# Two of three head-sum tiles added up before TensorE, and the rows of pi read back for two bands

## The chip, the cores and the metric

One core of one Trainium2 chip runs the whole problem in one launch. The metric is device time in microseconds, the median of three runs. A profiled execution shows what each engine did: PE (TensorE), DVE (VectorE), ACT (ScalarE), POOL (GpSimd) and SP (SyncE, which here issues most DMAs).

## The reference

```python
x = x + _L0_conv_ref(_gn(x), qkv_w, temp, out_w, out_b)   # x: (32, 384, 32, 32), 12 heads of 32 channels
...
    w = jnp.einsum('bnc,oc->bno', xt, qkv_w).reshape(b, n, HEADS, d).transpose(0, 2, 1, 3)
    norm = jnp.sqrt(jnp.sum(w * w, axis=-2, keepdims=True))
    w_normed = w / jnp.maximum(norm, 1e-12)
    s = jnp.sum(w_normed * w_normed, axis=-1)
    Pi = jax.nn.softmax(s * temp[None, :, :], axis=1)
    Pi_n = Pi / (jnp.sum(Pi, axis=-1, keepdims=True) + 1e-08)
    dots = jnp.einsum('bhn,bhnd->bhd', Pi_n, w * w)[:, :, None, :]
    attn = 1.0 / (1.0 + dots)
    out = -(w * Pi[..., None]) * attn
    out = jnp.einsum('bnc,oc->bno', out, out_w) + out_b
```

`_gn` is a group norm over 32 groups. For each image there are two products of 384 x 384 weights with 384 x 1024 values. Between them stands a softmax over the 12 heads at each of the 1024 positions. Its score of a head is the sum over the head's 32 channels of the squares, each channel's squares divided by their sum over the positions.

## The kernel before

The 32 images run one after the other in a software pipeline. An image's 384 channels are three tiles of 128 partitions (t = 0, 1, 2), each with 1024 positions in the free dimension. In each tile the 128 partitions are the 32 channels of four heads, so tile 0 holds heads 0 to 3, tile 1 heads 4 to 7 and tile 2 heads 8 to 11. Each product is written as three products of a high and a low part of weights and data (XH and XL, UH and UL, W1H and so on).

The order of the work is written out by hand: every engine has its own list of instructions, and semaphores hold them together. In `step(i)`:

- PE makes the three tiles of the first product of image i (`first_product`), then those of the second product of image i - 1 (`second_product`). `head_sums(i)` stands inside the second product of tile 0. It streams the squares of each tile against a column per head, `headsum[:, t, :]`, in four matmuls for the four quarters of the partitions of `scores`.
- ACT squares each tile of the first product (`square_w`, which also leaves the sums over the positions in `sumsq`), keeps the tile itself (`keep_w`), makes the high part of the weighed values of image i - 1 (`u_hi`) and normalises image i + 1 (`normalise`, `x_hi`).
- DVE first ends image i - 2 (`finish`, L1149), then works on image i - 1: three dot products (`dot`, L1041), the little chain of `attention` (L1053 and on), three weighings (`weigh`, L1067) and the low parts (`u_lo`, L1141). Then come the moments of the group norm of image i + 1 (L937), `head_sum_weights(i)` (L990 to L996), `group_norm`, the third `u_lo`, statistics (L906), the softmax of image i (L1005 to L1033) and the ends of image i - 1.
- SP stores image i - 2, loads image i + 2, and in `spread_pi(i)` sends the softmax out to DRAM and reads it back so that every partition has the rows of its head:

```python
                    for t in tiles:
                        rows = pi_dram[t * HPT:(t + 1) * HPT].rearrange("h (b q n) -> q (h b) n", b=BLOCKS, q=QUADS)
                        sp.dma_start(rows, PIT[:, t, :]).then_inc(pi_written[t], 16)
                    for t in tiles:
                        sp.wait_ge(pi_written[t], rows_moved(j, t, 16))
```

The writes are L375 and the reads, into PIB[:, t], L380. The dot products and the weighings of the next step use these rows. For the first and the last image the rows of tile 0 are spread by PE transposes instead (`spread_heads`), and the tiles are weighed one at a time (`attend_tile`, L1041, L1080, L1101).

Of the kernel before, what the change touches and what calls it, by code (L numbers as in the profile page):

```python
# [33 lines left out]
P = 128  # L34
# [6 lines left out]
QUAD = 32  # L41
# [4 lines left out]
BY_MATMUL = 3  # L46
HEADSUM_STEPS = 3
IDLE_TURNS = (4, 4)
SM_SHIFTED, SM_STEPS = 3, 8
ATTENDED = 3 + 4  # L50
U_STEPS = ATTENDED + 3
# [32 lines left out]
def conv_attention(nc, x, qkv_w, temp, out_w, out_b, y):  # L84
# [4 lines left out]
    T = C // P  # L89
    HPT = P // D  # L90
    HALVES = N // BANK
    BLOCKS = N // P
# [7 lines left out]
    with ExitStack() as ctx:  # L100
# [51 lines left out]
        srec = sb("srec", [P, BLOCKS])  # L152
        pi_part = sb("pi_part", [P, HPT])
        pi_heads = sb("pi_heads", [P, BLOCKS, HPT])
        PIT = sb("PIT", [P, T, QUAD + 1])
        PIB = sb("PIB", [P, T, BLOCKS * QUADS, QUAD + 1])
        pick = sb("pick", [P, T, HEADS])
# [45 lines left out]
        w_kept = sem("w_kept")  # L203
        headsum_step = sem("headsum_step")
        scores_done = sem("scores_done")
# [3 lines left out]
        pi_spread = [sem(f"pi_spread_{t}") for t in range(T)]  # L209
        u_step = sem("u_step")  # L210
# [50 lines left out]

        def rows_moved(j, t, more=0):

            return j.counts(16, more - (16 if t == 0 and True else 0))

# [74 lines left out]
        def _(sp):  # L340
# [67 lines left out]
        def _(pool):  # L408
# [6 lines left out]
            pool.wait_ge(w2_loaded, 16)  # L415
            pool.tensor_copy(mixed_w2.rearrange("p (m d h) -> p m d h", d=D, h=HPT),
                             raw_w2.rearrange("p (m h d) -> p m d h", d=D, h=HPT)).then_inc(w2_mixed, 1)

# [34 lines left out]
        def _(act):  # L453
# [83 lines left out]
            def widen_heads(j):  # L537

                act.wait_ge(heads_kept, pe_spread(j))
                if j.follows(1):  # L540
                    act.wait_ge(u_step, (j - 1).counts(U_STEPS, 1))
                act.activation(wide_heads(j).rearrange("p (b d h) -> p b d h", b=BLOCKS, d=D),
                               pi_heads[:].unsqueeze(2).to_broadcast([P, BLOCKS, D, HPT]), ACT.Copy)\
# [62 lines left out]
            def x_hi_first():  # L606
# [19 lines left out]
            act.wait_ge(u_step, last.counts(U_STEPS, 2 - U_STEPS))  # L626
            act.activation(wide_part(last).rearrange("p (d h) -> p d h", d=D),
                           pi_part[:].unsqueeze(1).to_broadcast([P, D, HPT]), ACT.Copy).then_inc(heads_widened, 1)
            u_hi(last, 0)
# [13 lines left out]
        def _(pe):  # L643
            def turn_weights(ks):
# [3 lines left out]
                for k in ks:  # L648
                    for m in range(T):
                        raw = columns1[:, k, m, :] if k < T else columns2[:, k - T, m, :]  # L650
                        if k < T:
                            into = turned(k)[:, m * P:(m + 1) * P].rearrange("p (d h) -> p h d", h=HPT)
# [136 lines left out]
            def head_sums(i):  # L789
# [5 lines left out]
                if i.follows(1):  # L795
                    pe.wait_ge(sm_step, i.counts(SM_STEPS))
                for t in range(T):
                    for q in range(QUADS):
                        block_q = square_tile(i, t).rearrange("p (b q r) -> p q b r", q=QUADS, r=QUAD)[:, q]
                        last = pe.matmul(scores[q * QUAD:(q + 1) * QUAD, 0:N // QUADS], headsum[:, t, :],  # L800
                                         block_q, start=(t == 0), stop=(t == T - 1))
                last.then_inc(scores_done, 1)
# [42 lines left out]
            def turn_w2():  # L845

                pe.wait_ge(w2_mixed, 1)
                pe.wait_ge(temp_kept, 1)
# [19 lines left out]
        def _(dve):  # L868
# [115 lines left out]
            def head_sum_weights(j):  # L984

                if not has(j):
                    return
                link = chain(headsum_step, j.counts(HEADSUM_STEPS))
                dve.wait_ge(squared, j.counts(T, T))
                link(dve.tensor_scalar(inv[:, 0, :], sumsq[:], NORM_FLOOR ** 2, None, ALU.max))  # L990
                link(dve.reciprocal(inv[:, 1, :], inv[:, 0, :]))
# [4 lines left out]
                link(dve.tensor_tensor(headsum[:], head_temp[:],  # L996
                                       inv[:, 1, :].unsqueeze(2).to_broadcast([P, T, QUAD]), ALU.mult), follows=False)

# [12 lines left out]
            def softmax_divide(j):  # L1011
# [7 lines left out]
                if by_pe(j):  # L1019
                    dve.tensor_tensor(pi_heads[:], EX[:, :, 0:HPT],  # L1020
                                      srec[:].unsqueeze(2).to_broadcast([P, BLOCKS, HPT]), ALU.mult).then_inc(heads_kept, 1)
                    if j.follows(1):
# [5 lines left out]
                if j.follows(1):  # L1028
                    for t in range(T):
                        if j.follows(2) or rows_moved(j, t) > 0:  # L1030
                            dve.wait_ge(pi_written[t], rows_moved(j, t))
                link(dve.transpose(PIT[:, :, 0:QUAD], scores[:, P:P + HEADS * BLOCKS]))
                link(dve.tensor_reduce(PIT[:, :, QUAD], PIT[:, :, 0:QUAD], AX_X, ALU.add), follows=False)  # L1033

            def dot(j, t):

                if has(j):
                    dve.wait_ge(pi_spread[t], rows_moved(j, t, 16))
                    dve.wait_ge(squared, j.counts(T, t + 1))
                    dve.wait_ge(scores_done, j.counts(1, 1))  # L1040
                    dve.tensor_tensor_reduce(in_blocks(square_tile(j, t)), PIB[:, t, :, 0:QUAD],  # L1041
                                             in_blocks(square_tile(j, t)), 1.0, 0.0,
                                             ALU.mult, ALU.add, dots[:, 0, t:t + 1]).then_inc(u_step, 1)

            def attention(j, k):
# [4 lines left out]
                if k > 0:  # L1050
                    dve.wait_ge(u_step, j.counts(U_STEPS, T + k))
# [10 lines left out]
            def weigh(j, t):  # L1062

                if has(j):
                    dve.wait_ge(u_step, j.counts(U_STEPS, ATTENDED))
                    dve.wait_ge(w_kept, j.counts(T, t + 1))
                    dve.scalar_tensor_tensor(in_blocks(w_tile(j, t)), in_blocks(w_tile(j, t)), dots[:, 3, t:t + 1],  # L1067
                                             PIB[:, t, :, 0:QUAD], ALU.mult, ALU.mult).then_inc(u_step, 1)

            def attend_tile(j, t, within=()):  # L1070
# [15 lines left out]
                else:  # L1086
                    rows = PIB[:, t, :, 0:QUAD]
                    dot(j, t)
                    dve.tensor_reduce(total, PIB[:, t, :, QUAD], AX_X, ALU.add).then_inc(tile_step, 1)
                for other in within:  # L1090
# [61 lines left out]
            def step(i):  # L1152
# [36 lines left out]
            def head_columns(t):  # L1189

                dve.tensor_reduce(head_mask[:, t, t * HPT:(t + 1) * HPT],
                                  identity[:].rearrange("p (d h) -> p h d", h=HPT), AX_X, ALU.add).then_inc(heads_set, 1)

# [83 lines left out]
```

## Time and profile before

| | |
|---|---|
| Time, median of 3 runs | 867.25 us (867.11 to 867.55) |
| Span of the profiled execution | 864.9 us |
| PE busy in it | 851.6 us (98%) |
| DVE busy | 750.2 us (87%) |
| ACT busy | 528.3 us (61%) |
| POOL busy | 232.6 us (27%) |
| TensorE clock granted | full speed in all 40 slices |

The span is the only time that the profile gives of the profiled execution: from its first to its last instruction. The time of a run is some 2.4 us longer than that span. Rows give the start and the duration in microseconds from the start of the span, and a name such as `WS<-PIB,WS` says which tile is written and which are read.

### The profile page before, as it was taken

How to read it: one execution, taken by the hardware profiler on the slowest of the kernel's cores; microseconds unless marked ns; L12 is line 12 of the kernel's file. 1: busy time of each engine (PE TensorE's matmuls, PEld its weight loads, DVE VectorE, ACT ScalarE, POOL GpSimd, SP SyncE). 2: the span in 40 equal slices, each digit the busy share in tenths (PEclk: the TensorE clock that was granted, in tenths of full speed). 3: DMA queues.
4: the chain of work that ended last, by engine and by line, in shares of the span. 5: the costliest groups of instructions: out<-in, count | busy, mean ns of one | idle time of the engine just before them, and what ended most of it. 6: DMA issues, size and time to landing. Idle time of an engine off the chain costs nothing.

```text
span 864.9 us, 14022 instructions
## 1 busy us (share of the span) xinstructions
PE 851.6 (98%) x4290; PEld 677.7 (78%) x4290; DVE 750.2 (87%) x1396; ACT 528.3 (61%) x680; POOL 232.6 (27%) x106
## 2 busy tenths in 40 slices
PE   7999999999999999999999999999999999999997
PEld 6767788777787777787777787777887777887776
DVE  7989889898888888888888898888898888898777
ACT  3567656567555677556676556676565675566642
POOL 2432123332123331133331233321233321233300
PEclk9999999999999999999999999999999999999999
DMA  7324665544664544664535654445655446645225
GB/s 279 119 79 153 225 229 185 185 148 169 225 227 161 197 146 181 226 223 160 180 150 198 228 213 168 163 145 220 227 186 196 141 163 225 228 175 186 88 86 197
DMA packets 45259, 157.42 MB, mean 182 GB/s; under 512 B 19866, under 2 KB 23962, under 8 KB 37274
## 3 DMA queue, kind: packets, MB, share of 16 engines
q1 hardware_dynamic: 36856, 154.10, 48.5%
q10 hardware_dynamic: 8354, 2.85, 1.3%
q14 instruction: 40, 0.33, 0.1%
q8 instruction: 9, 0.15, 0.1%
HBM read 104.47 MB, written 52.45 MB: 181 GB/s over the span
## 4 chain that ended last, share of the span: by engine, by line
PE 92%; DVE 4%; issue 1%; DMA 1%; ACT 1%; DVEq 0%; ACTq 0%
PE acc L678 86%; PE spread_ps L800 5%; DVE stats L906 1%; DVE WS L1041 1%; DMA PIB<-pi 0%; DMA X<-in_x 0%; DVE WV L1101 0%; DVE X L1149 0%; PE acc L655 0%; DVE WS L1080 0%; ACT WS L501 0%; DMA pi<-PIT 0%; DVE X L1116 0%; ACT WV L512 0%; PE spread_ps L815 0%
## 5 line engine op out<-in xcount | busy, mean ns | idle before, releaser
L424 POOL TENSOR_TENSOR XL<-XN,XH 128x1024 fp32r<-128x1024 f32 x93 | 222.9, 2414 | 571.7 <-ACT XH L529 548.2
L501 ACT ACTIVATE WS<-acc 128x1024 f32<-128x1024 f32 x96 | 98.4, 1026 | 240.5 <-PE acc L678 197.1
L678 PE MATMUL acc<-XH,W1H 128*128 128x512 f32 x574 | 177.3, 390 | 0.1
L678 PE MATMUL acc<-XH,W1L 128*128 128x512 f32 x574 | 176.8, 389 | 0.0
L678 PE MATMUL acc<-UH,W2H 128*128 128x512 f32 x558 | 172.6, 390 | 1.3 <-ACT WV L512 1.2
L678 PE MATMUL acc<-UH,W2L 128*128 128x512 f32 x558 | 172.3, 390 | 0.0
L678 PE MATMUL acc<-XL,W1H 128*128 128x512 f32 x576 | 146.2, 389 | 0.0
L678 PE MATMUL acc<-UL,W2H 128*128 128x512 f32 x558 | 145.3, 396 | 0.0
L1149 DVE SCALAR_TENSOR_TENSOR X<-acc,bias,X 128x1024 f32<-128x1024 f32 x93 | 116.3, 1276 | 31.0 <-PE acc L678 31.0
L678 PEld LDWEIGHTS acc<-UL,W2H 128*128 128x128 f32 x558 | 102.3, 188 | 32.2 <-issue 11.9
L678 PEld LDWEIGHTS acc<-XL,W1H 128*128 128x128 f32 x576 | 108.0, 188 | 22.7 <-POOL XL L434 0.3
L678 PEld LDWEIGHTS acc<-XH,W1L 128*128 128x128 f32 x574 | 107.7, 188 | 22.5
L678 PEld LDWEIGHTS acc<-XH,W1H 128*128 128x128 f32 x574 | 107.3, 188 | 23.0 <-issue 0.9
L678 PEld LDWEIGHTS acc<-UH,W2H 128*128 128x128 f32 x558 | 104.3, 188 | 24.9 <-issue 2.1
L1041 DVE CUSTOM_DVE_ANT_0 WS<-PIB,WS 128x1024 f32<-128x1024 f32 x94 | 113.5, 1222 | 10.2 <-DMA PIB<-pi 8.1
L906 DVE BATCH_NORM_STATS2 stats<-X 128x6 f32<-128x512 f32 x192 | 120.0, 680 | 2.5 <-DMA X<-in_x 2.5
L678 PEld LDWEIGHTS acc<-UH,W2L 128*128 128x128 f32 x558 | 104.6, 188 | 22.4 <-issue 0.4
L491 ACT ACTIVATE UH<-WV 128x1024 fp32r<-128x1024 f32 x93 | 95.0, 1054 | 41.7 <-DVE WV L1067 37.5
L519 ACT ACTIVATE XN<-X,norm 128x1024 f32<-128x1024 f32 x91 | 112.3, 1235 | 0.4 <-DVE XN L961 0.4
L1141 DVE TENSOR_TENSOR UL<-WV,UH 128x1024 fp32r<-128x1024 f32 x93 | 111.2, 1222 | 0.1
L1067 DVE SCALAR_TENSOR_TENSOR WV<-WV,dots,PIB 128x1024 f32<-128x1024 f32 x90 | 110.3, 1281 | 1.1
L529 ACT ACTIVATE XH<-X,norm 128x1024 fp32r<-128x1024 f32 x90 | 111.0, 1233 | 0.0
(119 smaller groups left out, 501.3 us busy)
## 6 DMA issues: line engine op xcount, KB each, us to landing
PIB<-pi SPq DMA_DIRECT2D x94, 528.0 KB, 5.1
X<-in_x SPq DMA_DIRECT2D x31, 1536.0 KB, 6.3
out_y<-X SPq DMA_DIRECT2D x30, 1536.0 KB, 6.5
gathered<-stats_rows ACTq DMA_DIRECT2D x28, 72.0 KB, 5.1
pi<-PIT SPq DMA_DIRECT2D x94, 16.5 KB
X<-in_x SPq DMA_DIRECT2D x3, 512.0 KB, 4.7
out_y<-X SPq DMA_DIRECT2D x1, 1024.0 KB, 6.0
out_y<-X SPq DMA_DIRECT2D x2, 512.0 KB, 2.6
```

What stands on the lines that cost most here:

```text
L424: pool.tensor_tensor(XL[:, t, :], XN[:, t, :], XH[:, t, :].bitcast(F32), ALU.subtract).then_inc(xl_done, 1)
L491: act.activation(u_tiles(j)[0][:, t, :], w_tile(j, t), ACT.Copy).then_inc(uh_done, 1)
L501: act.activation(square_tile(i, t), acc[:, t, :], ACT.Square, accum_out=sumsq[:, t:t + 1]).then_inc(squared, 1)
L519: act.activation(XN[:, t, :], x_tile(j, t), ACT.Identity, bias=shift_j, scale=rstd_j).then_inc(xn_done, 1)
L529: act.activation(XH[:, t, :], x_tile(j, t), ACT.Identity, bias=shift_j, scale=rstd_j).then_inc(xh_done, 1)
L678: last = pe.matmul(out[:, h * BANK:(h + 1) * BANK], w[:, k, m * P:(m + 1) * P], r[:, k, h * BANK:(h + 1) * BANK], start=(n == 0 and k == 0 ...
L800: last = pe.matmul(scores[q * QUAD:(q + 1) * QUAD, 0:N // QUADS], headsum[:, t, :], block_q, start=(t == 0), stop=(t == T - 1))
L906: last = dve.bn_stats(stats[:, k, :], X[:, j.slot, k * BANK:(k + 1) * BANK])
L1041: dve.tensor_tensor_reduce(in_blocks(square_tile(j, t)), PIB[:, t, :, 0:QUAD], in_blocks(square_tile(j, t)), 1.0, 0.0, ALU.mult, ALU.add, ...
L1067: dve.scalar_tensor_tensor(in_blocks(w_tile(j, t)), in_blocks(w_tile(j, t)), dots[:, 3, t:t + 1], PIB[:, t, :, 0:QUAD], ALU.mult, ALU.mult ...
L1141: dve.tensor_tensor(low[:, t, :], w_tile(j, t), high[:, t, :].bitcast(F32), ALU.subtract).then_inc(ul_done[t], 1)
L1149: dve.scalar_tensor_tensor(x_tile(j, t), acc[:, t, :], bias[:, t:t + 1], x_tile(j, t), ALU.add, ALU.add).then_inc(y_done, 1)
```

## The change

In every image from the third on, the squares of tiles 0 and 1 are added up before PE sees them, each scaled by the inverse of its channel's sum (`inv`). For this the two tiles get one common layout, in which the 128 partitions are 16 channels of eight heads in each tile ("band 0", heads 0 to 7), so that a partition belongs to the same head in both. Tile 2 stays as it is ("band 1"). The columns of the first and the rows of the second weight matrix are reordered at the start to suit.

- DVE makes the scales of tiles 0 and 1 early (`pair_weights`, after the three weighings).
- ACT writes scaled squares of tile 0 to a new tile `paired` (`scale_first`, ahead of the third square).
- DVE adds the scaled squares of tile 1 (`add_second`, after `group_moments` and ahead of `head_sum_weights`, which is left with tile 2).
- PE streams `paired` and tile 2: eight matmuls in the code instead of twelve.
- SP writes the softmax out in three DMAs as before, but reads it back in two: one for band 0, once writes 0 and 1 have landed, and one for band 1. Tiles 0 and 1 use the same rows.
- The sum over the rows in `attention` becomes two instructions. In the first and last image PE spreads eight heads instead of four, and all three tiles are written out.

```diff
                     sp.wait_ge(sm_step, j.counts(SM_STEPS, SM_STEPS))
-                    tiles = range(1 if by_pe(j) else 0, T)
-                    for t in tiles:
+                    for t in range(T):
                         rows = pi_dram[t * HPT:(t + 1) * HPT].rearrange("h (b q n) -> q (h b) n", b=BLOCKS, q=QUADS)
                         sp.dma_start(rows, PIT[:, t, :]).then_inc(pi_written[t], 16)
-                    for t in tiles:
-                        sp.wait_ge(pi_written[t], rows_moved(j, t, 16))
-                        heads = pi_dram[t * HPT:(t + 1) * HPT].unsqueeze(0)\
-                            .to_broadcast([D, HPT, BLOCKS * QUADS * (QUAD + 1)])
-                        sp.dma_start(PIB[:, t].rearrange("p b n -> p (b n)"), heads).then_inc(pi_spread[t], 16)
+                    for band, of_band in enumerate(BAND_HEADS):
+                        for t in range(of_band.start // HPT, of_band.stop // HPT):
+                            sp.wait_ge(pi_written[t], j.counts(16, 16))
+                        heads = pi_dram[of_band.start:of_band.stop].unsqueeze(0)\
+                            .to_broadcast([P // len(of_band), len(of_band), BLOCKS * QUADS * (QUAD + 1)])
+                        sp.dma_start(PIB[:, band].rearrange("p b n -> p (b n)"), heads).then_inc(pi_spread[band], 16)
...
+            def scale_first(i):
+
+                if has(i):
+                    act.wait_ge(headsum_step, i.counts(HEADSUM_STEPS, 2))
+                    act.wait_ge(squared, i.counts(T, 1))
+                    act.wait_ge(scores_done, i.counts(1))
+                    act.activation(paired[:], square_tile(i, 0), ACT.Copy, scale=inv[:, 1, 0:1]).then_inc(pair_step, 1)
...
                 square_w(i, 1)
                 u_hi(i - 1, 1)
                 u_hi(i - 1, 2)
+                scale_first(i)
                 square_w(i, 2)
...
-                for t in range(T):
+                if paired_sums(i):
+                    pe.wait_ge(pair_step, i.counts(PAIR_STEPS, PAIR_STEPS - PAIR_STEPS * PAIRED))
+                    streams = [(head_temp[:, 0, :], paired[:]), (headsum[:, T - 1, :], square_tile(i, T - 1))]
+                else:
+                    streams = [(headsum[:, t, :], square_tile(i, t)) for t in range(T)]
+                for n, (weights, squares) in enumerate(streams):
...
+            def pair_weights(j):
+
+                if not has(j):
+                    return
+                link = chain(headsum_step, j.counts(HEADSUM_STEPS))
+                dve.wait_ge(squared, j.counts(T, 2))
+                dve.wait_ge(scores_done, j.counts(1))
+                link(dve.tensor_scalar(inv[:, 0, 0:2], sumsq[:, 0:2], NORM_FLOOR ** 2, None, ALU.max))
+                link(dve.reciprocal(inv[:, 1, 0:2], inv[:, 0, 0:2]), follows=False)
+
+            def add_second(j):
+
+                if not has(j):
+                    return
+                dve.wait_ge(pair_step, j.counts(PAIR_STEPS, 1 - PAIR_STEPS * PAIRED))
+                dve.scalar_tensor_tensor(paired[:], square_tile(j, 1), inv[:, 1, 1:2], paired[:], ALU.mult, ALU.add)\
+                    .then_inc(pair_step, 1)
...
-                    dve.wait_ge(pi_spread[t], rows_moved(j, t, 16))
+                    dve.wait_ge(pi_spread[BAND[t]], j.counts(16, 16))
...
-                    done = dve.tensor_reduce(total, PIB[:, :, :, QUAD], AX_X, ALU.add)
+                    dve.tensor_reduce(total[:, 0:2], PIB[:, 0, :, QUAD].unsqueeze(1).to_broadcast([P, 2, BLOCKS * QUADS]),
+                                      AX_X, ALU.add).then_inc(u_step, 1)
+                    done = dve.tensor_reduce(total[:, 2:3], PIB[:, 1, :, QUAD], AX_X, ALU.add)
...
                 weigh(i - 1, 2)
+                pair_weights(i)
                 u_lo(i - 1, 0)
                 u_lo(i - 1, 1)
                 group_moments(i + 1)
+                add_second(i)
                 head_sum_weights(i)
```

## Rows read from the trace of the kernel before

**Rows 1.** The page, busy time of each engine.

```profile
PE 851.6 (98%) x4290; PEld 677.7 (78%) x4290; DVE 750.2 (87%) x1396; ACT 528.3 (61%) x680; POOL 232.6 (27%) x106
```

**Rows 2.** The chain that ended last, 400 to 455 us: start, us, what.

```profile
416.72 1.43 PE spread_ps L800 x24
418.15 24.72 PE acc L678 x108
```

**Rows 3.** Waits of DVE, 89 to 796 us: total us, times, longest.

```profile
DVE X L1149 <- PE acc L678: 24.9, 28, 0.9
DVE inv L990 <- ACT WS L501: 19.6, 23, 1.0
...
DVE WS L1041 <- DMA PIB<-pi: 8.1, 16, 1.0
```

**Rows 4.** Timeline of DVE: first dots of images 1, 2, 29; end of a softmax.

```profile
64.88 1.22 DVE L1041 CUSTOM_DVE_ANT_0 WS<-PIB,WS 128x1024 f32<-128x1024 f32 x1
...
82.67 0.26 DVE L1033 TENSOR_REDUCE PIT<-PIT 128x3 f32<-128x96 f32 x1
...
89.16 1.22 DVE L1041 CUSTOM_DVE_ANT_0 WS<-PIB,WS 128x1024 f32<-128x1024 f32 x1
...
795.30 1.22 DVE L1041 CUSTOM_DVE_ANT_0 WS<-PIB,WS 128x1024 f32<-128x1024 f32 x1
```

**Rows 5.** Timeline of SP's DMA issues, image 2.

```profile
82.95 1.71 SPq L375 DMA_DIRECT2D pi<-PIT  x3
85.11 1.89 SPq L380 DMA_DIRECT2D PIB<-pi  x3
```

**Rows 6.** Landing of single first reads at 85.1, 424.5, 790.6 us; of all reads.

```profile
PIB<-pi SPq DMA_DIRECT2D x1, 528.0 KB, 4.0
...
PIB<-pi SPq DMA_DIRECT2D x1, 528.0 KB, 4.2
...
PIB<-pi SPq DMA_DIRECT2D x1, 528.0 KB, 4.3
...
DMA to landing us min/median/max: 3.8/5.1/6.8
```

**Rows 7.** Timeline of DVE, 407 to 418 us.

```profile
407.71 3.68 DVE L1067 SCALAR_TENSOR_TENSOR WV<-WV,dots,PIB 128x1024 f32<-128x1024 f32 x3
...
411.30 2.35 DVE L1141 TENSOR_TENSOR UL<-WV,UH 128x1024 fp32r<-128x1024 f32 x2
...
415.34 0.17 DVE L990 TENSOR_SCALAR inv<-sumsq 128x3 f32<-128x3 f32 x1 [0.96 <-ACT WS L501]
...
415.54 0.18 DVE L991 RECIPROCAL inv<-inv 128x3 f32<-128x3 f32 x1
...
416.84 0.21 DVE L953 TENSOR_SCALAR norm<-group_mv,norm 128x1 f32<-128x1 f32 x1
...
417.01 1.23 DVE L1141 TENSOR_TENSOR UL<-WV,UH 128x1024 fp32r<-128x1024 f32 x1
```

**Rows 8.** Groups by line and shape: busy us, mean ns | idle before.

```profile
L1053 DVE TENSOR_REDUCE pi_tot<-PIB 128x3 f32<-128x96 f32 x30 | 9.9, 331 | 0.0
...
L1089 DVE TENSOR_REDUCE pi_tot<-PIB 128x1 f32<-128x32 f32 x4 | 0.8, 207 | 0.0
...
L491 ACT ACTIVATE UH<-WV 128x1024 fp32r<-128x1024 f32 x93 | 95.0, 1054 | 41.7 <-DVE WV L1067 37.5 <-DVE WV L1101 4.2
...
L519 ACT ACTIVATE XN<-X,norm 128x1024 f32<-128x1024 f32 x91 | 112.3, 1235 | 0.4 <-DVE XN L961 0.4
```

**Rows 9.** Timeline of ACT, 411 to 415 us.

```profile
411.13 2.00 ACT L491 ACTIVATE UH<-WV 128x1024 fp32r<-128x1024 f32 x2
...
414.19 1.03 ACT L501 ACTIVATE WS<-acc 128x1024 f32<-128x1024 f32 x1 [1.07 <-PE acc L678]
```

**Rows 10.** Timeline of DVE, the last image: end of softmax, dot of tile 1.

```profile
839.08 0.26 DVE L1033 TENSOR_REDUCE PIT<-PIT 128x3 f32<-128x96 f32 x1
...
845.71 1.21 DVE L1041 CUSTOM_DVE_ANT_0 WS<-PIB,WS 128x1024 f32<-128x1024 f32 x1
```

More of the change, by code:

```diff
@@ L46 @@
 BY_MATMUL = 3
-HEADSUM_STEPS = 3
+HEADSUM_STEPS = 5
+PAIR_STEPS = 2
+PAIRED = 2
+BAND = (0, 0, 1)
+BANDS = 2
 IDLE_TURNS = (4, 4)
 SM_SHIFTED, SM_STEPS = 3, 8
-ATTENDED = 3 + 4
+ATTENDED = 3 + 5
 U_STEPS = ATTENDED + 3
@@ L90, in conv_attention @@
     HPT = P // D
+    PAIR_HEADS = 2 * HPT
+    PAIR_D = P // PAIR_HEADS
+    BAND_HEADS = (range(0, PAIR_HEADS), range(PAIR_HEADS, HEADS))
     HALVES = N // BANK
@@ L152, in conv_attention @@
         srec = sb("srec", [P, BLOCKS])
-        pi_part = sb("pi_part", [P, HPT])
-        pi_heads = sb("pi_heads", [P, BLOCKS, HPT])
+        pi_part = sb("pi_part", [P, PAIR_HEADS])
+        pi_heads = sb("pi_heads", [P, BLOCKS, PAIR_HEADS])
+        paired = sb("paired", [P, N])
         PIT = sb("PIT", [P, T, QUAD + 1])
-        PIB = sb("PIB", [P, T, BLOCKS * QUADS, QUAD + 1])
+        PIB = sb("PIB", [P, BANDS, BLOCKS * QUADS, QUAD + 1])
         pick = sb("pick", [P, T, HEADS])
@@ L204, in conv_attention @@
         headsum_step = sem("headsum_step")
+        pair_step = sem("pair_step")
         scores_done = sem("scores_done")
@@ L208, in conv_attention @@
         pi_written = [sem(f"pi_written_{t}") for t in range(T)]
-        pi_spread = [sem(f"pi_spread_{t}") for t in range(T)]
+        pi_spread = [sem(f"pi_spread_{band}") for band in range(BANDS)]
         u_step = sem("u_step")
@@ L260, in pe_spread, with band_rows, paired_sums @@
             return 2 if j.follows(1) else 1
-        def rows_moved(j, t, more=0):
-            return j.counts(16, more - (16 if t == 0 and True else 0))
+        def band_rows(t):
+            return PIB[:, BAND[t], :, 0:QUAD]
+        def paired_sums(j):
+            return j.follows(PAIRED)
         def tile_steps(j, t, steps):
@@ L415, in _ @@
             pool.wait_ge(w2_loaded, 16)
-            pool.tensor_copy(mixed_w2.rearrange("p (m d h) -> p m d h", d=D, h=HPT),
-                             raw_w2.rearrange("p (m h d) -> p m d h", d=D, h=HPT)).then_inc(w2_mixed, 1)
+            for band in BAND_HEADS:
+                columns, h = slice(band.start * D, band.stop * D), len(band)
+                pool.tensor_copy(
+                    mixed_w2.rearrange("p (t c) -> p t c", t=T)[:, :, columns].rearrange("p t (d h) -> p t d h", h=h),
+                    raw_w2.rearrange("p (t c) -> p t c", t=T)[:, :, columns].rearrange("p t (h d) -> p t d h", h=h))\
+                    .then_inc(w2_mixed, 1)
             def x_lo(j, t):
@@ L626, in _ @@
             act.wait_ge(u_step, last.counts(U_STEPS, 2 - U_STEPS))
-            act.activation(wide_part(last).rearrange("p (d h) -> p d h", d=D),
-                           pi_part[:].unsqueeze(1).to_broadcast([P, D, HPT]), ACT.Copy).then_inc(heads_widened, 1)
+            act.activation(wide_part(last).rearrange("p (d h) -> p d h", d=PAIR_D),
+                           pi_part[:].unsqueeze(1).to_broadcast([P, PAIR_D, PAIR_HEADS]), ACT.Copy).then_inc(heads_widened, 1)
             u_hi(last, 0)
@@ L651, in turn_weights @@
                         if k < T:
-                            into = turned(k)[:, m * P:(m + 1) * P].rearrange("p (d h) -> p h d", h=HPT)
+                            band = BAND_HEADS[m * HPT // PAIR_HEADS]
+                            heads = slice(m * HPT - band.start, (m + 1) * HPT - band.start)
+                            into = turned(k)[:, band.start * D:band.stop * D].rearrange("p (d h) -> p h d", h=len(band))[:, heads]
                         else:
@@ L796, in head_sums @@
                     pe.wait_ge(sm_step, i.counts(SM_STEPS))
-                for t in range(T):
+                if paired_sums(i):
[4 more added lines that the diff above has]
+                for n, (weights, squares) in enumerate(streams):
                     for q in range(QUADS):
-                        block_q = square_tile(i, t).rearrange("p (b q r) -> p q b r", q=QUADS, r=QUAD)[:, q]
-                        last = pe.matmul(scores[q * QUAD:(q + 1) * QUAD, 0:N // QUADS], headsum[:, t, :],
-                                         block_q, start=(t == 0), stop=(t == T - 1))
+                        block_q = squares.rearrange("p (b q r) -> p q b r", q=QUADS, r=QUAD)[:, q]
+                        last = pe.matmul(scores[q * QUAD:(q + 1) * QUAD, 0:N // QUADS], weights, block_q,
+                                         start=(n == 0), stop=(n == len(streams) - 1))
                 last.then_inc(scores_done, 1)
@@ L845, in turn_w2 @@
             def turn_w2():
[L847 removed]
+                pe.wait_ge(w2_mixed, BANDS)
                 pe.wait_ge(temp_kept, 1)
@@ L987, in head_sum_weights @@
                     return
-                link = chain(headsum_step, j.counts(HEADSUM_STEPS))
+                tiles = slice(T - 1, T) if paired_sums(j) else slice(0, T)
+                done = HEADSUM_STEPS - 3 if paired_sums(j) else 0
+                link = chain(headsum_step, j.counts(HEADSUM_STEPS, done))
                 dve.wait_ge(squared, j.counts(T, T))
-                link(dve.tensor_scalar(inv[:, 0, :], sumsq[:], NORM_FLOOR ** 2, None, ALU.max))
-                link(dve.reciprocal(inv[:, 1, :], inv[:, 0, :]))
+                link(dve.tensor_scalar(inv[:, 0, tiles], sumsq[:, tiles], NORM_FLOOR ** 2, None, ALU.max))
+                link(dve.reciprocal(inv[:, 1, tiles], inv[:, 0, tiles]))
                 if j.follows(1):
@@ L995, in head_sum_weights @@
                     dve.wait_ge(temp_kept, 3)
-                link(dve.tensor_tensor(headsum[:], head_temp[:],
-                                       inv[:, 1, :].unsqueeze(2).to_broadcast([P, T, QUAD]), ALU.mult), follows=False)
+                weights = headsum[:, tiles, :]
+                dve.tensor_tensor(weights, head_temp[:, tiles, :], inv[:, 1, tiles].unsqueeze(2).to_broadcast(weights.shape),
+                                  ALU.mult).then_inc(headsum_step, HEADSUM_STEPS - 2 - done)
+            def pair_weights(j):
[12 more added lines that the diff above has]
+                    .then_inc(pair_step, 1)
             def softmax_shift(j):
@@ L1086, in attend_tile @@
                 else:
-                    rows = PIB[:, t, :, 0:QUAD]
+                    rows = band_rows(t)
                     dot(j, t)
-                    dve.tensor_reduce(total, PIB[:, t, :, QUAD], AX_X, ALU.add).then_inc(tile_step, 1)
+                    dve.tensor_reduce(total, PIB[:, BAND[t], :, QUAD], AX_X, ALU.add).then_inc(tile_step, 1)
                 for other in within:
```

22 lines of the change are left out of this document (11 added, 11 removed).

## The prediction

> **What bounds the kernel now.** I read four views. First the busy line of the page: the matmul engine (PE) is busy for 851.6 of 864.9 us, DVE for 750.2 [rows 1]. Second the chain of work that ended last, over two periods of the loop: it is PE alone, 1.43 us of head sums and 24.72 us of products, which makes a period of 26.15 us [rows 2]. The first dot product on DVE is at 89.16 for image 2 and at 795.30 for image 29 [rows 4]: 706.14 us / 27 = 26.15 as well. So whatever shortens PE shortens the kernel, as long as nothing else needs 26.15 us.
>
> Third, therefore, what DVE waits for in those 27 periods [rows 3]. It idles 24.9 us for PE before the last store tile and 19.6 us for ACT's third square before the head sum weights. These 44.5 us, 1.65 a period, are real slack. But 16 times it also idles for the rows of pi that come back from DRAM: those rows already arrive only just in time. That is a second loop beside PE's: dot products, weighing, head sum weights, softmax, rows written out, rows read back, dot products of the next image.
>
> Fourth, that loop measured by itself. One period shows its DVE part with no wait for PE, ACT or DMA ahead of the head sum weights: from the first dot at 64.88 to the end of the last softmax reduction at 82.67 + 0.26 = 82.93 [rows 4], so 18.05 us. Behind it the writes are issued at 82.95, the first read at 85.11 [rows 5], it lands 4.0 us later [rows 6], and the dot starts at 89.16 [rows 4]. Loop: 18.05 + 6.23 = 24.28 us against 26.15. The slack is 1.87 us, and what the change adds to this loop is to be held against it.
>
> **The change part by part.** *PE.* 24 head sum records take 1.43 us [rows 2], three tiles of eight; one tile goes, 1.43 / 3 = 0.48 us. PE's period would be 25.67. All 30 paired images together could give 14.3 us.
>
> *ACT.* scale_first writes 128x1024 from SBUF. The plain copy of that shape takes 1.05 us, the one with scale and bias operands 1.24 [rows 8]; I take 1.1. It stands where ACT now idles 1.07 us before the third square (copies end at 411.13 + 2.00, the square starts at 414.19) [rows 9], so it costs nothing on the path. If it ran 0.2 over, the third square would be as late, and behind it the seeds and w copies; DVE reaches the weights later than before anyway (below), which covers that.
>
> *DVE, pair_weights.* Two small linked instructions after the last weighing: 0.20 from the first to the second (415.34 to 415.54), and from a small one to the next subtraction 0.17 (416.84 to 417.01) [rows 7]. 0.37 us; bounds 0.30 (some of it overlapped) and 0.45 (a wait instruction not hidden). Its wait for the second square is met: ACT squares tile 1 right after copying the first weighed tile, 1 us each, while DVE still weighs two tiles. Behind pair_weights stand the two subtractions, and scale_first waits for it too.
>
> *DVE, add_second.* Same instruction and shape as the weighing: three take 411.30 - 407.71 = 3.59, so 1.20 us [rows 7] (1.28 if nothing overlaps). Behind it in DVE's order are the head sum weights, the group norm, the third subtraction and the softmax, so all of it is in the loop.
>
> *DVE, small ones.* The reduction of totals becomes two, of 64 and 32 elements instead of 96. 96 take 0.33, 32 take 0.21 [rows 8]: I take +0.07; bounds nothing and a whole instruction, 0.21. The weights of one tile instead of three go from 96 to 32 elements, which in the reductions is worth 0.12 [rows 8]; I take -0.07, bounds -0.10 and 0.
>
> Sum on DVE: 0.37 + 1.20 + 0.07 - 0.07 = 1.57 us; bounds 1.40 and 1.94. That alone is most of the 1.87.
>
> *The rows.* Three writes stay. The reads become two of the same 528 KB. The third read disappears, which helps only the third dot: the first dot, which starts the chain, now waits for band 0, and SP may issue that only after writes 0 **and** 1. Writes go out 1.71 / 3 = 0.57 to 0.6 us apart [rows 5], so the first read leaves 0.6 us later than now: 85.11 - 82.93 = 2.18 becomes 2.78 (bounds 2.75, and 2.87 if SP needs a further wait instruction). From issue to landing the first read of an image took 4.0, 4.2 and 4.3 us in the first, 14th and last of 28 periods [rows 6]; the mean of the 28 is 4.1. With 0.02 to the dot, the way from softmax to first dot is 2.78 + 4.1 + 0.02 = 6.90 us, against 6.23 in the measured period. Bounds: 2.75 + 3.8 (the least of all reads [rows 6]) + 0.02 = 6.57, and 2.87 + 4.3 + 0.02 = 7.19.
>
> On this price the Trainium skill would come out otherwise. Its page "DMA: Bandwidth & Descriptors", section "Anatomy of one DMA", fits a transfer as 2.0 us plus its bytes at 436 GB/s, fitted on the GpSimd path, while this read is SP's. For 528 KB that is an estimate of 3.24 us; the trace does not agree, with 4.0 to 4.3 [rows 6], and the measurement decides.
>
> *Start and end.* The weights' copy in two pieces, the strided transposes and the head masks move the same elements once; one more instruction is worth 0.2 [rows 8], and I take nothing. The last image has tile 1 waiting for band 0: now its dot starts at 845.71, 6.37 us after 839.34 [rows 10], and 6.8 to 6.9 are needed, so +0.5. Image 29 to 30 has no statistics to make, and runs at PE's shorter period, -0.5; the last head sums give 0.4 back. Together -0.4.
>
> **The sum.** Let s be what DVE adds plus the way of the rows: 1.57 + 6.90 = 8.47. The loop's period is 18.05 + 8.47 = 26.52 us, longer than PE's 25.67 and than today's 26.15. PE then idles 0.85 us an image at the head sums. The first dot of image 2 moves from 89.16 to 64.88 + 26.52 = 91.40, +2.24; 27 periods give 27 x (26.52 - 26.15) = +10.0; the ends -0.4. Total +11.8. In general: (s - 6.23) + 27 (s - 8.10) - 0.4. On the profiled execution that is 864.9 + 11.8 = 876.7 of span; the median of the runs, 867.25, lies 2.4 above that span, which I take as unchanged: 879.
>
> Bounds: s = 1.40 + 6.57 = 7.97 gives -2.2, 865; s = 1.94 + 7.19 = 9.13 gives +30.3, 897.6.
>
> **The rivals.**
>
> 1. *The second write costs nothing* (other side: faster). If band 0 lands when the first read lands today, 6.25 us behind the softmax, s is 7.82 and the loop 25.87: 1.6 - 7.6 - 0.4 = -6.4, 861. It decides from s = 8.05, that is from a way below 6.5 us; below 6.05 PE at 25.67 is the bound again. For it: the stretch before the landing is the same, and if something other than the issue set it, the issue would not move it. Against: 4.0 to 4.3 us from issue in three periods [rows 6], so the issue moves the landing. Chance 0.10. The page of the Trainium skill named above belongs here: with its estimate of 3.24 us the way would be 6.04, s 7.61 and the time 855.
>
> 2. *No change*, s between 7.99 and 8.11: small instructions overlap and the read takes its least. Chance 0.07.
>
> 3. *The read also slows down*. The median over all reads is 5.1 us [rows 6], because second and third reads queue behind the first; if band 0 met other traffic the same way, the way is 2.87 + 5.1 + 0.02 = 7.99, s = 9.56: 3.3 + 39.4 - 0.4 = +42, 910. For it: period and traffic shift against each other. Against: still first in its queue, and the store of an image is issued only after the reads. Chance 0.08.
>
> 4. The forecast, a loop through DVE and the rows that ends up longer than PE's: 0.75.
>
> **The range.** From 865, the lower bound, to 896, just under the upper: the faster rival and the slow read, 0.18 together, are left out. Within 0.2% is 1.7 us, about what a measurement of this kernel can tell from no change. Slower 0.83, within it 0.07, faster 0.10.
>
> **What the profile after would show.** Head sums of 16 records an image instead of 24. First dots 26.5 us apart. DVE idle before the *first* dot of each image, about 1 us, released by the DMA of the rows, and none before the third. Idle time before the weights on DVE gone. PE idle before the head sums, some 0.85 us an image, released by DVE's weights or the added tile. The reads issued 2.8 us after the softmax and landing 4.1 later. ACT's third square not later than the end of the addition on DVE. The forecast is wrong if the first dot waits for nothing, or if the additions on DVE sum to under 1.4 or over 1.95 us.

## The result and the profile after

The changed kernel takes 899.1 us (898.7 to 899.9) where the kernel before takes 867.4: 1.036 times as long, 95% interval 1.035 to 1.038. The sign and the mechanism were as forecast, the size was not: +31.7 us, where +11.8 was worked out, and 899 lies above the range of 865 to 896.

The busy line of the changed kernel answers to [rows 1]: PE has less work, 845.0 us, in a longer span.

```profile
span 896.9 us, 13948 instructions
...
PE 845.0 (94%) x4050; PEld 668.3 (75%) x4050; DVE 789.7 (88%) x1516; ACT 558.8 (62%) x710; POOL 232.7 (26%) x107
```

The chain that ended last, by engine, is no longer PE alone. DVE's work and the transfers of the rows make up 62% of it, and most of the rest is time in which the engine waited for nothing that the profile shows (`issue`).

```profile
DVE 39%; issue 24%; DMA 23%; PE 6%; ACT 3%; SPq 2%; DVEq 2%; POOL 0%; ACTq 0%; POOLq 0%
```

The waits from 92 to 828 us, which are 27 periods, answer to [rows 3] (engine and line, waited for: total us, times, longest). First DVE's, then PE's.

```profile
DVE WS L1094 <- DMA PIB<-pi: 39.0, 28, 1.7
DVE X L1204 <- PE acc L706: 10.6, 28, 1.5
DVE ssum L1071 <- ACT spread_ps L552: 8.7, 27, 0.3
...
DVE UL L1196 <- issue: 2.2, 6, 0.4
DVE PIT L1085 <- DVE spread_ps L1080: 1.4, 6, 0.2
```

```profile
PE spread_ps L833 <- DVE headsum L1032: 33.7, 26, 2.3
```

PE now idles 33.7 / 27 = 1.25 us a period at the head sums, for DVE. DVE idles 39.0 us for the rows, in every period; before, it was 8.1 us. DVE's wait for ACT's third square, 19.6 us before, is gone.

The timeline of DVE answers to [rows 4 and 7]: the first dots of images 2 and 29, and between them one whole period of image 14 to 15.

```profile
92.54 1.23 DVE L1094 CUSTOM_DVE_ANT_0 WS<-PIB,WS 128x1024 f32<-128x1024 f32 x1
...
419.80 1.23 DVE L1094 CUSTOM_DVE_ANT_0 WS<-PIB,WS 128x1024 f32<-128x1024 f32 x1 [1.56 <-DMA PIB<-pi]
...
423.24 0.28 DVE L1106 TENSOR_REDUCE pi_tot<-PIB 128x2 f32<-128x64 f32 x1
423.43 0.21 DVE L1108 TENSOR_REDUCE pi_tot<-PIB 128x1 f32<-128x32 f32 x1
423.67 0.16 DVE L1110 SCALAR_TENSOR_TENSOR dots<-pi_tot,dots 128x3 f32<-128x3 f32 x1
...
427.87 0.16 DVE L1042 TENSOR_SCALAR inv<-sumsq 128x2 f32<-128x2 f32 x1
428.06 0.17 DVE L1043 RECIPROCAL inv<-inv 128x2 f32<-128x2 f32 x1
428.23 2.36 DVE L1196 TENSOR_TENSOR UL<-WV,UH 128x1024 fp32r<-128x1024 f32 x2
...
431.24 1.22 DVE L1050 SCALAR_TENSOR_TENSOR paired<-WS,inv,paired 128x1024 f32<-128x1024 f32 x1
432.37 0.15 DVE L1025 TENSOR_SCALAR inv<-sumsq 128x1 f32<-128x1 f32 x1
...
432.86 0.21 DVE L977 TENSOR_SCALAR scaled<-group_mv,seed 128x1 f32<-128x1 f32 x1
...
438.16 0.27 DVE L1080 TENSOR_TENSOR spread_ps<-spread_ps,srec 128x96 f32<-128x96 f32 x1
438.46 0.28 DVE L1085 STREAM_TRANSPOSE PIT<-spread_ps 128x96 f32<-128x96 f32 x1
438.77 0.26 DVE L1086 TENSOR_REDUCE PIT<-PIT 128x3 f32<-128x96 f32 x1
...
446.56 1.23 DVE L1094 CUSTOM_DVE_ANT_0 WS<-PIB,WS 128x1024 f32<-128x1024 f32 x1 [1.11 <-DMA PIB<-pi]
...
827.30 1.23 DVE L1094 CUSTOM_DVE_ANT_0 WS<-PIB,WS 128x1024 f32<-128x1024 f32 x1 [1.51 <-DMA PIB<-pi]
```

From image 2 to image 29 the period is (827.30 - 92.54) / 27 = 27.21 us, where 26.52 was forecast. In the period shown, DVE's part runs from 419.80 to 438.77 + 0.26 = 439.03, 19.23 us (forecast 19.62). The way of the rows runs from 439.03 to 446.56, 7.53 us (forecast 6.90). Over the 28 periods the way is 7.79 us on average.

SP's issues behind that softmax answer to [rows 5], and the landing of two single reads for band 0, in images 14 and 15, to [rows 6].

```profile
439.06 1.70 SPq L387 DMA_DIRECT2D pi<-PIT  x3
441.84 1.22 SPq L393 DMA_DIRECT2D PIB<-pi  x2
```

```profile
PIB<-pi SPq DMA_DIRECT2D x1, 528.0 KB, 4.8
...
PIB<-pi SPq DMA_DIRECT2D x1, 528.0 KB, 4.5
```

The read leaves 2.81 us after the softmax, as forecast (2.78). But it lands 4.8 and 4.5 us later in these two images, 4.76 on the mean of 28 (4.5 to 5.1), where the first read of an image took 4.1 before the change.

### The profile page after: what moved, and what is told of

Read it like the earlier page. It is cut to its first block, busy times and chain, and to the rows that moved or that the text cites. A ratio compares the mean times of both kernels' runs of the same rounds, so it can differ in the third digit from the quotient of the medians.

```text
span 896.9 us, 13948 instructions
## 1 busy us (share of the span) xinstructions
PE 845.0 (94%) x4050; PEld 668.3 (75%) x4050; DVE 789.7 (88%) x1516; ACT 558.8 (62%) x710; POOL 232.7 (26%) x107
## 4 chain that ended last, share of the span: by engine, by line
DVE 39%; issue 24%; DMA 23%; PE 6%; ACT 3%; SPq 2%; DVEq 2%; POOL 0%; ACTq 0%; POOLq 0%
DMA PIB<-pi 16%; DMA pi<-PIT 7%; DVE WV L1122 7%; PE acc L706 5%; DVE UL L1196 5%; DVE WS L1094 5%; DVE stats L939 4%; SPq L387 2%; DVE paired L1050 1%; DVE spread_ps L1059 1%; ACT UH L508 1%; DVE PIT L1085 1%; DVE spread_ps L1080 1%; DVE ssum L1071 1%; DVE smax L1060 1%
## 5 line engine op out<-in xcount | busy, mean ns | idle before, releaser
L706 PE MATMUL acc<-UL,W2H 128*128 128x512 f32 x558 | 149.2, 403 | 0.0
L1094 DVE CUSTOM_DVE_ANT_0 WS<-PIB,WS 128x1024 f32<-128x1024 f32 x94 | 110.5, 1223 | 40.3 <-DMA PIB<-pi 40.3
L706 PEld LDWEIGHTS acc<-UL,W2H 128*128 128x128 f32 x558 | 100.5, 189 | 38.0 <-issue 12.3
```

The source lines that it names most:

```text
L706: last = pe.matmul(out[:, h * BANK:(h + 1) * BANK], w[:, k, m * P:(m + 1) * P], r[:, k, h * BANK:(h + 1) * BANK], start=(n == 0 and k == 0 ...
L1094: dve.tensor_tensor_reduce(in_blocks(square_tile(j, t)), band_rows(t), in_blocks(square_tile(j, t)), 1.0, 0.0, ALU.mult, ALU.add, dots[:, ...
```

## The experiments

Each run was compared with the kernel before on its own chip (867.2 to 868.0 us there). "Landing" is the mean time from issue to landing of the read for band 0 over 28 images, and "way" that from the end of the softmax to the first dot. A period is the mean time from one image's first dot to the next one's, over the 27 periods from image 2 to image 29, and DVE's part is the period less the way.

**Four rows in the read.**

```diff
-                        heads = pi_dram[of_band.start:of_band.stop].unsqueeze(0)\
-                            .to_broadcast([P // len(of_band), len(of_band), BLOCKS * QUADS * (QUAD + 1)])
+                        heads = pi_dram[of_band.start:of_band.start + HPT].unsqueeze(0)\
+                            .to_broadcast([D, HPT, BLOCKS * QUADS * (QUAD + 1)])
```

> The changed kernel, but the read for band 0 takes rows 0 to 3, each for 32 partitions, in place of rows 0 to 7, each for 16; both writes are still waited for, and as many bytes land in as many pieces. Tiles 0 and 1 are so weighed with the wrong rows; only the time counts. Theory A (in the changed kernel band 0's read takes 4.7 us from issue to landing instead of 4.1 because of its pattern of eight rows): landing 4.1 after issue, periods 0.65 us shorter, some 29 of them, 899 - 19 = 880 us. Rival B (it is late because of what else the DMA engines carry at that time, the statistics and their gather, which now come before it): still 4.7, and 899 us.

885.4 us, 1.019 (1.017 to 1.022), and landing 4.0 us. A single one, issued at the same 2.8 us after the softmax:

```profile
PIB<-pi SPq DMA_DIRECT2D x1, 528.0 KB, 4.1
```

The statistics and their gather are where they were, and the read is quick again, so B falls. The pattern of the read is a cause by itself, worth 13.8 us. That is less than the 19 expected, since every fourth period stays at 27.5 to 30.5 us, while all others have 26.1 to 26.5. In the images that begin these six periods the third dot waits for band 1's rows and starts 2.9 to 4.2 us after the first, where it starts 2.3 us after it in all others. The third dot of image 5:

```profile
174.77 1.23 DVE L1094 CUSTOM_DVE_ANT_0 WS<-PIB,WS 128x1024 f32<-128x1024 f32 x1 [1.79 <-DMA PIB<-pi]
```

**Rows 4 to 7 instead.** The same edit with `pi_dram[of_band.stop - HPT:of_band.stop]`.

> The changed kernel, but the read for band 0 takes rows 4 to 7, each for 32 partitions, in place of rows 0 to 7, each for 16 (the tiles are weighed with wrong rows, only the time counts). It tells two readings of the run with rows 0 to 3 apart, which landed 4.0 us after issue. Theory A (eight different rows in one read are what is slow): rows 4 to 7 land as early as rows 0 to 3, 4.0 to 4.1 us after issue, and the time is that run's, 883 to 887 us. Theory C (rows 4 to 7 are slow because the write that made them has only just landed when the read is issued, while rows 0 to 3 are 0.6 us older): landing 4.7 us after issue and 899 us.

888.3 us, 1.024 (1.022 to 1.025), landing 4.25 us on the mean: 4.0 to 4.4 in 24 images, 4.8 to 4.9 in four. Nearer to A than to C, so the age of the rows is not the main thing, but the time lies just above A's 883 to 887.

**Each row for 16 neighbours.**

```diff
-                        heads = pi_dram[of_band.start:of_band.stop].unsqueeze(0)\
-                            .to_broadcast([P // len(of_band), len(of_band), BLOCKS * QUADS * (QUAD + 1)])
+                        if band == 0:
+                            heads = pi_dram[of_band.start:of_band.stop].unsqueeze(1)\
+                                .to_broadcast([len(of_band), P // len(of_band), BLOCKS * QUADS * (QUAD + 1)])
+                        else:
+                            heads = pi_dram[of_band.start:of_band.stop].unsqueeze(0)\
+                                .to_broadcast([P // len(of_band), len(of_band), BLOCKS * QUADS * (QUAD + 1)])
```

> The changed kernel, but the read for band 0 takes rows 0 to 7 in another order: each row for 16 neighbouring partitions, in place of rows 0 to 7 over and over (tiles 0 and 1 are weighed with wrong rows, only the time counts). Theory A1 (the read is slow because neighbouring pieces, which one DMA engine moves, are of eight different rows): 4.1 us from issue to landing, and 883 to 889 us. Theory A2 (it is slow because eight rows in all are touched, in whatever order): 4.7 us and 897 to 900 us.

997.6 us, 1.150 (1.148 to 1.152): landing 7.9 us. The timeline of DVE in this kernel, from the end of a softmax to the first dot:

```profile
451.26 0.25 DVE L1090 TENSOR_REDUCE PIT<-PIT 128x3 f32<-128x96 f32 x1
...
462.61 1.23 DVE L1098 CUSTOM_DVE_ANT_0 WS<-PIB,WS 128x1024 f32<-128x1024 f32 x1 [4.89 <-DMA PIB<-pi]
```

Neither A1's 4.1 us nor A2's 4.7 came out, but the run does not decide between them, because it changed more than the order. The read's access pattern now begins with a count of 8 where it had 16, and the trace points to half of the 16 DMA engines. For this read it holds 16 landing marks in the changed kernel, in image 14 at 4.5 to 4.8 us after the issue. Here it holds nine in every image, in image 14 one at 1.0 us, before the first piece has moved, and eight at 7.1 to 8.1. These are the stretches from 2 to 4 us after the issue in image 14, first in the changed kernel, then in this one; the last but one number is the busy share of the DMA engines (records of transfers overlap, so it can pass 1).

```profile
416.79:418.79 2.00, 2.00 (x11) 1.65 (x9) 1.28 (x1) 0.00 (x0) 0.80 (x1) 1.00 1.02 268
456.33:458.33 2.00, 2.00 (x11) 1.65 (x10) 1.28 (x1) 0.00 (x0) 0.76 (x1) 1.00 0.50 146
```

Over the 28 images the share is 1.02 on the mean and 0.69 here, with the read for band 1 beside it. That the order alone makes a read slow is therefore not shown.

**The rows waited for last.**

```diff
-                    dve.wait_ge(pi_spread[BAND[t]], j.counts(16, 16))
                     dve.wait_ge(squared, j.counts(T, t + 1))
                     dve.wait_ge(scores_done, j.counts(1, 1))
+                    dve.wait_ge(pi_spread[BAND[t]], j.counts(16, 16))
```

> The changed kernel, with the three waits of a dot product in another order: the rows of pi are waited for last. Theory: in the changed kernel the first dot starts 0.2 us after its rows have landed, because two more waits stand behind that wait as instructions of their own; with the rows last it starts 0.02 to 0.05 after, 29 periods give 5 us, 894 us. Rival (the 0.2 us are the landing's own): no change, 899 us.

898.4 us, 1.036 (1.034 to 1.037): no difference from the changed kernel that shows. The mechanism was there: the first dot starts 0.03 us after the landing instead of 0.22. But the landing itself was later, 4.88 us instead of 4.76, so the way fell by only 0.08 us. The expected 5 us are not to be had in this way; why the landing moved is open.

**One column of the addition.** Of the addition, `paired[:, 0:1]` alone is done.

> The changed kernel, but the addition of tile 1 on DVE does one column of 1024; the other sums lack tile 1, and the scores are not the reference's. Theory (the loop through DVE and the rows sets the period, and the addition lies in it with 1.13 us): about 1.0 us less a period, 26.2 us, and 899 - 28 = 870 us. Rival (the addition is not in the loop that counts, for instance because the waits for PE or ACT take its place): 890 us or more.

879.8 us, 1.013 (1.011 to 1.015). The addition is in the loop, but 0.60 us a period came back instead of 1.0 (period 26.61). Two things took its place: DVE's part fell only to 18.65 us, with a new wait for ACT's third square behind the short addition, and the landing was 4.94 us.

```profile
423.52 0.15 DVE L1050 SCALAR_TENSOR_TENSOR paired<-WS,inv,paired 128x1 f32<-128x1 f32 x1
423.91 0.15 DVE L1025 TENSOR_SCALAR inv<-sumsq 128x1 f32<-128x1 f32 x1 [0.24 <-ACT WS L518]
```

**The rows for two bands alone.**

```diff
-            return j.follows(PAIRED)
+            return False
...
-                scale_first(i)
...
-                pair_weights(i)
...
-                add_second(i)
```

> One part of the change alone: the layout of eight heads and the reads for two bands, with the head sums of three tiles as before (nothing scaled on ACT, nothing added on DVE); it computes the reference. Theory (loop of DVE and rows): 18.05 us of DVE and 7.8 us from the softmax to the first dot make 25.85 us, under PE's 26.15, so PE sets the period again and the time is that of before, 867 to 869 us. Rival (the later rows cost something by themselves, whatever DVE does): 875 us or more.

869.0 us, 1.0016 (1.0006 to 1.0026), period 26.15. The read lands 4.92 us after its issue here too, with nothing scaled or added. A way of 7.99 us costs 1 us by itself as long as DVE's part is 18 us; it makes the kernel slow only once DVE's part has grown.

**Band 0 in two reads.** The eight heads get another order of partitions, so that four rows fill 64 partitions:

```diff
-                    for band, of_band in enumerate(BAND_HEADS):
-                        for t in range(of_band.start // HPT, of_band.stop // HPT):
-                            sp.wait_ge(pi_written[t], j.counts(16, 16))
-                        heads = pi_dram[of_band.start:of_band.stop].unsqueeze(0)\
-                            .to_broadcast([P // len(of_band), len(of_band), BLOCKS * QUADS * (QUAD + 1)])
-                        sp.dma_start(PIB[:, band].rearrange("p b n -> p (b n)"), heads).then_inc(pi_spread[band], 16)
+                    for t in range(T):
+                        sp.wait_ge(pi_written[t], j.counts(16, 16))
+                        band, of_band = BAND[t], BAND_HEADS[BAND[t]]
+                        copies = P // len(of_band)
+                        first = (t * HPT - of_band.start) * copies
+                        heads = pi_dram[t * HPT:(t + 1) * HPT].unsqueeze(0)\
+                            .to_broadcast([copies, HPT, BLOCKS * QUADS * (QUAD + 1)])
+                        sp.dma_start(PIB[first:first + copies * HPT, band].rearrange("p b n -> p (b n)"), heads)\
+                            .then_inc(pi_spread[band], 16)
```

> The change with another layout of the eight heads: heads 0 to 3 on partitions 0 to 63, heads 4 to 7 on 64 to 127. The rows for band 0 come in two reads of 264 KB, four rows each for 16 partitions, the first issued after write 0 alone; it computes the reference. Theory (the way from the softmax to the first dot sets the period, and both the late issue and the pattern are in it): the first half leaves 2.2 us after the softmax, the second 2.8, and both have landed some 3.6 us later, at 6.4 to 6.6 instead of 7.6; 1.0 to 1.2 us a period less, 866 to 871 us. Rival (a read's time is a fixed part, whatever its size, and pattern of 16 copies is slow as such): the second half lands at 7.4 or later, 890 us or more.

878.9 us, 1.013 (1.011 to 1.015). Between the two: both halves had landed 6.87 us after the softmax, the second 4.07 after its issue though it has half the bytes. This is the landing that the forecast had taken for the read (2.78 + 4.1), and the time is the forecast's 879. In part that is luck: the first dot starts only 7.13 us after the softmax, 0.23 later than forecast, and DVE's part, 19.42 us, is 0.20 shorter.

**Tile 2 ahead.** Writes, reads and dots in the order 2, 0, 1.

```diff
-                for t in range(T):
+                for t in (2, 0, 1):
                     dot(i - 1, t)
```

> The changed kernel with tile 2 ahead: its rows are written and read first, and its dot product comes first; it computes the reference. Theory: the first dot starts 6.3 us after the softmax, as before the change, and works 1.15 us while band 0 comes in; band 0, now behind in the queue, lands at 8.2 to 8.7, so the three dots end 0.3 to 0.7 us earlier than at 11.26 in the changed kernel: 880 to 892 us. Rival (band 0's read is delayed by as much as the dot of tile 2 takes): no change, 899 us.

914.8 us, 1.055 (1.053 to 1.057), against both theory and rival. The first dot starts at 6.7 us, but write 1 is now the last, so the read for band 0 leaves 3.3 us or more after the softmax and lands at 9.2; the dots end later than before. I had left out that a write moved back holds the read that waits for it.

**Both together.**

> The layout with two half reads and tile 2 ahead, both together; it computes the reference. Theory: tile 2's dot starts at 6.3 us, the halves land at 7.0 and 7.6, the dots end at about 10 us as with the halves alone or slightly earlier: 862 to 870 us. Rival: the halves, last in the queue, land after 8.5 us and the time is that of tile 2 ahead alone, 880 us or more.

893.4 us, 1.031 (1.030 to 1.033). The rival holds in the main: the halves land 8.46 us after the softmax, and the time is above 880.

**The statistics after the softmax.**

```diff
-                group_stats(i + 2, [0])
                 softmax_shift(i)
                 softmax_divide(i)
-                group_stats(i + 2, range(1, T))
+                group_stats(i + 2, range(T))
```

> The changed kernel with one piece of DVE's other work moved: the first two statistics instructions of image i + 2 (1.2 us), now between the third subtraction and the softmax, come after the softmax, where DVE idles 1.1 to 1.6 us for the rows; it computes the reference. Theory (a loop of 19.2 us of DVE and 7.8 us of rows sets the period): the DVE part falls to 18.05, the period from 27.2 to 26.0 to 26.2 us, 866 to 872 us. Rival (the scores are not ready earlier, since PE's head sums wait for the added tile; DVE idles in front of the softmax instead): 890 us or more.

872.8 us, 1.006 (1.005 to 1.008), period 26.3: 26 us less than the changed kernel, for a move of 1.2 us of DVE's work out of its part of the loop into its wait for the rows. DVE's wait for them falls from 39.0 to 12.8 us. The theory's 866 to 872 was missed by 0.8 us.

**The same move in the kernel before.**

> The kernel before the change, with the same two statistics instructions moved after the softmax; it computes the reference. Theory (before the change PE sets the period, and the loop of DVE and rows has slack): no change, 866.5 to 868.5 us, so that a gain in the two runs beside this one is not the move's alone. Rival (the rows that come just in time cost something before the change too): 3 us or more faster.

866.9 us, 0.999 (0.998 to 1.000): no change, as PE set the period.

**Two reads, the statistics after the softmax and the rows waited for last.**

> The layout with two half reads (878.9 us), the statistics after the softmax, and the rows waited for last in a dot product; it computes the reference. Theory: DVE 18.05 and the way of the rows 6.9 make 24.95 us, so PE with 25.67 us and its small waits is the bound again: 855 to 863 us, faster than before the change. Rival (DVE's whole work, 25.4 us a period with its links, and PE's waits for it do not fit together): 866 us or more.

861.3 us, 0.993 (0.991 to 0.995): 0.7% faster than the kernel before. Three things were changed at once here, and what each gives in their company was not separated. The chain of this kernel is PE's again, and PE waits 1.3 us for DVE in 27 periods where it was 33.7.

```profile
391.83 24.85 PE acc L714 x108
416.68 1.00 PE spread_ps L841 x16
```

```profile
PE spread_ps L841 <- DVE headsum L1040: 1.3, 6, 0.2
```

## Why the prediction was wrong in size

**The bound.** Right. The loop through DVE and the rows of pi set the period in place of PE. The runs show it apart from the sum: less DVE work in the loop (the move of the statistics) gives back 26 us, a quicker read 11 to 20, and the rows alone, with DVE's part short, cost 1.

**PE and ACT.** As forecast: 16 head sum records an image, and scale_first is 1.14 us long (1.1 taken) and hidden. PE's gain shows in the last run, where PE sets the period again: 16 head sum records take 1.00 us there against 1.43 for 24, 0.43 less where 0.48 was taken, and the period is 25.85 us (25.67 taken). With a longer loop the gain only lengthens PE's wait.

**DVE's additions.** Mis-sized, to the other side. 1.57 us were taken; the period shown has 19.23 - 18.05 = 1.18, below the lower bound of 1.40. The forecast had named additions under 1.4 us as a sign of being wrong. These rows of the kernel before, from the period of 18.05 us, are to be held against the period shown above:

```profile
68.31 0.33 DVE L1053 TENSOR_REDUCE pi_tot<-PIB 128x3 f32<-128x96 f32 x1
68.67 0.16 DVE L1055 SCALAR_TENSOR_TENSOR dots<-pi_tot,dots 128x3 f32<-128x3 f32 x1
...
75.87 0.10 DVE L990 TENSOR_SCALAR inv<-sumsq 128x3 f32<-128x3 f32 x1
...
76.55 0.21 DVE L944 TENSOR_SCALAR scaled<-group_mv,seed 128x1 f32<-128x1 f32 x1
...
81.86 0.27 DVE L1026 TENSOR_TENSOR spread_ps<-spread_ps,srec 128x96 f32<-128x96 f32 x1
82.35 0.28 DVE L1032 STREAM_TRANSPOSE PIT<-spread_ps 128x96 f32<-128x96 f32 x1 [0.23 <-DVE spread_ps L1026]
```

pair_weights is 428.23 - 427.87 = 0.36 (0.37 taken), and the addition 432.37 - 431.24 = 1.13 (1.20, priced from the weighing, whose operand has rows with gaps). The two reductions take 0.43 up to the next instruction where the one took 0.36, so +0.07 as taken. The weights of one tile take 0.49 where those of three took 0.68: -0.19 (-0.07 taken, bound -0.10). The last 0.19 stood in no term. The transpose behind the softmax starts 0.30 us after the instruction before it, where it started after 0.49 in 28 of the 32 images of the kernel before; in the changed kernel that gap is left only where the loop's body starts over. 0.36 + 1.13 + 0.07 - 0.19 - 0.19 = 1.18. The prediction would have been nearer to no change by this alone, 0.39 us a period.

**The way of the rows.** This step failed, and in it the price of the read. The issue was right, 2.82 us on the mean (2.78 taken). The landing was taken over from the first read of an image, 4.1 us, as if a read of 528 KB cost the same whichever rows it reads. The read of eight rows takes 4.76, +0.66 us; with four rows it was 4.0 at the same place. The dot's start was taken 0.02 us after the landing and is 0.22; with the rows waited for last it is 0.03. Together 7.79 us instead of 6.90, +0.89; the bounds ended at 7.19. The row "3.8/5.1/6.8" of [rows 6] did hold such times, but I had put all of them down to queueing behind an earlier read. Rival 3 thus had the right place with the wrong reason, since the read is slow while still the first of its image, and its price of 5.1 was too high.

**The rest.** DVE's part is 27.21 - 7.79 = 19.42 us on the mean and 19.23 in the period shown. Most of the 0.19 comes with six periods of the 27, every fourth, in which the loop's body of four images starts over; those are 27.4 to 28.3 us long. Most of that is the wait of the subtraction for nothing that the profile shows, 2.2 us in six times, and the gap before the transpose, 1.4 us in six times. Why they come there was not followed further.

So 26.52 - 0.39 + 0.89 + 0.19 = 27.21 us, the measured period. 27 x 0.69 = 18.6 us, 1.1 more up to the first dot of image 2 (92.54, forecast 91.40), and the ends, which gave nothing back where 0.4 was taken (69.6 us from the first dot of image 29 to the end of the span, before and after), are the 20.1 us between 879 and 899.

**The rivals.** That the second write costs nothing fell: the read leaves when both writes have landed. The page of the Trainium skill named there, "DMA: Bandwidth & Descriptors", section "Anatomy of one DMA", by whose fit for the GpSimd path 528 KB take an estimate of 3.24 us, is off by more for this read of SP's than before, with 4.76 us measured.

## What to carry to other kernels

Before work is taken off the engine that sets the period, measure the next loop by itself, from an event to the same event of the next round, with the transfers in it; here its slack was 1.87 us, and the change took 1.18 on DVE and 1.56 on the way of the rows. A broadcast read is to be priced from a read of the same pattern, not only of the same size. And where an engine waits on a loop's transfer, work that can stand in that wait is to be moved out of the loop's other part: the move alone took the change from 3.6% slower to 0.6%, and together with two reads of four rows and the rows waited for last it made the kernel 0.7% faster than before.

## What the runs showed of the hardware that was not expected

The time of one read of 528 KB from DRAM to 128 partitions, issued 2.8 us after the softmax in every case, by the rows that it takes: 4.0 us for four rows in turn (rows 0 to 3), 4.25 for rows 4 to 7, 4.76 for eight rows in turn. The cause of these differences is open. The 7.9 us for eight rows, each 16 times in a row, are another matter: that read shows nine landing marks in place of 16, and a smaller share of the DMA engines at work.

In the changed kernel the first dot starts 0.22 us after the landing in 27 of 28 images, and with the rows waited for last 0.03 on the mean. The order written in the code is not the whole of it: the kernel before writes the rows' wait first too, and its third dots start 0.02 us after the landing in 22 of 28 images and 0.22 in six. In the images looked at, the trace shows the rows' wait as an instruction of its own with a second wait behind it where the start is late, and as a wait of the dot itself where it is early. It did not show in the time.

In every fourth image an 8 KB instruction fetch falls among the softmax's writes, and the second read, which waits for the third write, leaves 0.5 to 0.8 us later (in the image below 2.01 us for both issues, against 1.22 in the one above). That the one holds the other back was not tested. These are also the images whose third dot waited in the run with rows 0 to 3. SP's reads of one such image in the timeline of the changed kernel:

```profile
387.29 2.01 SPq L393 DMA_DIRECT2D PIB<-pi  x2
```
